# Six stacked layers on one core: keys ahead of the norm spreads, the hidden products a slot later, GELU behind both squares

## The reference, cut to what matters

```python
def attn_layer(x, Wqkv, qs, ksc, Wo):          # 16 heads of 64, windows of 32 keys
    q, k, v = split(x @ Wqkv)
    q = l2norm(q) * qs; k = l2norm(k) * ksc
    q, k = rotary(q), rotary(k)                 # k with the inverse scale
    sim = q @ k.T * 8, this window and the one before, masked
    return softmax(sim) @ v @ Wo
def ffn_layer(x, g, bln, W1, b1, W2, b2):
    xn = (x - mean) / sqrt(var + 1e-5) * g + bln
    a, gate = split(xn @ W1 + b1)               # 341 columns each, padded to 3 x 128
    return a * gelu(gate) @ W2 + b2
x = attn_layer(shift_tokens(x)) + x
x = ffn_layer(shift_tokens(x)) + x
```

## Time and profile before

| | |
|---|---|
| median of 3 runs | 4278.9 us (4273.93 to 4289.5) |
| profiled execution, own time | 4266.5 us |
| its span | 4264.8 us, mean granted TensorE clock 0.96 |
| TensorE matmul busy | 3939.0 us (92%) |
| VectorE busy | 3159.2 us (74%) |
| ScalarE busy | 3038.3 us (71%) |
| GpSimd busy | 1809.0 us (42%) |

### The profile page before, as it was taken

The page is one execution under the profiler, slowest core; times in us unless marked ns, Lnnn a source line. Parts: engine busy times, 40 slices in busy tenths (PEclk is TensorE's granted clock), DMA queues, the critical chain, the costliest instruction groups (busy, mean ns, idle before and its releaser), DMA issues. The chain is left out here.

```text
span 4264.8 us, 112685 instructions
## 1 busy us (share of the span) xinstructions
PE 3939.0 (92%) x43857; PEld 2386.4 (56%) x43857; DVE 3159.2 (74%) x4169; ACT 3038.3 (71%) x7076; POOL 1809.0 (42%) x1071
## 2 busy tenths in 40 slices
PE   7997999999999999999967589999999999999997
PEld 3443666656555655556536446565566565665664
DVE  5774878878877877778735478778778787887785
ACT  3555777777778777777762267787777777777876
POOL 3112444444444444444404534444444444444442
PEclk8998999999999999999986699999999999999999
DMA  2212444444444444444300044444444444444442
GB/s 44 32 22 74 104 112 104 109 106 99 110 104 95 113 103 103 108 103 103 75 11 3 3 122 108 111 96 114 104 95 111 100 109 98 107 107 103 96 103 50
DMA packets 232525, 380.84 MB, mean 89 GB/s; under 512 B 59364, under 2 KB 122336, under 8 KB 231688
## 3 DMA queue, kind: packets, MB, share of 16 engines
q1 hardware_dynamic: 231560, 372.20, 37.5%
q10 hardware_dynamic: 384, 0.79, 0.1%
HBM read 39.22 MB, written 1.05 MB: 9 GB/s over the span
## 5 line engine op out<-in xcount | busy, mean ns | idle before, releaser
L839 POOL TENSOR_TENSOR b_roll<-b_roll,b_sws 128x1024 f32<-128x1024 f32 x384 | 910.1, 2370 | 1741.0 <-DMA b_sws<-b_roll 1741.0
L1205 DVE SCALAR_TENSOR_TENSOR b_roll<-ps,b_qks,b_rot 128x1024 f32<-128x1024 f32 x768 | 956.3, 1278 | 109.5 <-ACT b_sq L1135 72.3
L1120 ACT ACTIVATE b_prob<-ps,b_nmx 128x96 f32<-128x96 f32 x3072 | 756.0, 374 | 0.7 <-DVE b_nmx L1226 0.2
L1253 DVE TENSOR_TENSOR b_roll<-b_roll,ps 128x512 f32<-128x512 f32 x384 | 264.1, 688 | 503.1 <-PE ps L942 498.0
L844 POOL TENSOR_TENSOR b_prob<-b_prob,b_rinv 128x768 f32<-128x768 f32 x384 | 566.1, 1474 | 119.7 <-DVE b_rinv L1267 118.6
L881 PEld LDWEIGHTS ps<-ident,b_prob 128*128 128x128 f32 x3072 | 381.4, 142 | 309.6 <-issue 254.2
L881 PE MATMUL ps<-ident,b_prob 128*128 128x128 f32 x3072 | 468.3, 275 | 49.9 <-issue 28.4
L1072 ACT ACTIVATE b_pT<-ps 128x512 f32<-128x512 f32 x768 | 488.5, 636 | 29.1 <-PE ps L881 28.5
L1012 PE MATMUL ps<-b_wqkv,b_xs 128*128 128x256 f32 x1536 | 408.3, 388 | 35.0 <-DVE b_roll L1205 34.9
L934 PE MATMUL ps<-b_oT,b_wo 128*128 128x512 f32 x768 | 405.7, 610 | 14.7 <-ACT b_oT L1087 12.0
L903 PEld LDWEIGHTS ps<-b_pT,b_vs 128*64 128x64 f32 x6144 | 310.1, 137 | 184.2 <-issue 159.9
(11 more groups left out here) (290 smaller groups left out, 6956.9 us busy)
## 6 DMA issues: line engine op xcount, KB each, us to landing
b_sws<-b_roll SPq DMA_DIRECT2D x1536, 128.0 KB, 2.3
b_vs<-b_va SPq DMA_DIRECT2D x384, 256.0 KB, 3.8
b_wqkv<-in_L_ffn_Wqkv SPq DMA_DIRECT2D x96, 192.0 KB, 3.6
b_xs<-y SPq DMA_DIRECT2D x126, 128.0 KB, 2.3
b_wo<-in_L_ffn_Wo SPq DMA_DIRECT2D x96, 64.0 KB, 3.2
b_xs<-y SPq DMA_DIRECT2D x42, 127.8 KB, 2.4
b_rot<-in_rot SPq DMA_DIRECT2D x2, 2048.0 KB, 8.0
b_w<-in_L_ffn_W SPq DMA_DIRECT2D x24, 170.5 KB
```

The costliest lines, as they stand in the source:

```text
L839: pool.tensor_tensor(prc[:, r, :, :], prc[:, r, :, :], sws[:, r % 2, :, :], ALU.add)\
L1120: g = act.activation(prob[:, kc, i, P - KEYS:P], wide[0][:, h * CH + m * KEYS:h * CH + (m + 1) * KEYS], ACT.Exp, bias=nmx[:, kc % 2, i:i + 1])
L1205: dve.scalar_tensor_tensor(out=two_runs((2 * r + i) * CH, (8 + 2 * (r % 2) + i) * CH), in0=both, scalar=scale, in1=rot[:, 2 * i:2 * i + 2, ...
```

## The change

It moves work between places in the order of each engine; no operation is added or taken away, and every shape stays.

- TensorE: the keys of a come right after Wo, ahead of the two spreads, and the queries after the spreads. The spread for q goes to bank 2 and that for k to bank 7, where before they went to banks 1 and 2. The strips go to bank 2 instead of bank 6. The hidden products a (L965) run in steps 3 to 5 instead of 2 to 4; the products g stay in 2 to 4.
- ScalarE: the square of the keys comes before that of the queries, both behind the exponentials and ahead of the second transposes and of the GELU. The square for the variance, the second half of the LayerNorm's inverse root, and the bias of the normalised input move behind the exponentials.
- VectorE: the sum of the probabilities and its reciprocal move from the end of a slot to the start of the next; the hidden bias add goes between them and the rotary products; the sum into y moves ahead of the normalised q; the normalised input of the feed-forward comes last.

```diff
@@ TensorE @@
-                    if step in (2, 3, 4):
-                        pe.wait_ge(S["f_acp"], ONE + FT * C + step - 1)
+                    if step in (3, 4, 5):
+                        pe.wait_ge(S["f_acp"], ONE + FT * C + step - 2)
...
-                def strips(U, d, pe=pe):
+                def strips(U, b, pe=pe):
                     pe.wait_ge(S["sqk_done"], ONE + U + 1)
-                    if d:
-                        pe.wait_ge(S["pt_cp"], ONE + 2 * um(d)[0] + 2)
+                    pe.wait_ge(S["sqq_done"], ONE + U + 1)
+                    if b:
+                        pe.wait_ge(S["qn_done"], ONE + um(b)[0] + 1)
                     for s in range(4):
-                        m = pe.matmul(bank[6][32 * s:32 * s + 32, :], head_of[:, :], sq[:, s, :],
+                        m = pe.matmul(bank[2][32 * s:32 * s + 32, :], head_of[:, :], sq[:, s, :],
...
+                        if p:
+                            pe.wait_ge(S["pk_done"], ONE + um(p)[0] + 1)
+                        pe.matmul(bank[1][:, :], W[:, 1, :], X, start=True, stop=True).then_inc(S["k_mm"], 1)
+                    if b:
+                        UB, kb = um(b)
+                        pe.wait_ge(S["split_done"], ONE + twos(b) + 1)
+                        key_bank_free(f0)
+                        if j % 2 == 0 and p:
+                            pe.wait_ge(S["ln_done"], ONE + twos(p) + 1)
+                        pe.matmul(bank[2][:, :], take[:, 2 * (kb % 2), :], rsp[:, :], start=True, stop=True)
+                        if e:
+                            pe.wait_ge(S["y_add"], ONE + UE + 1)
+                        pe.matmul(bank[7], take[:, 2 * (kb % 2) + 1, :], rsp[:, :], start=True, stop=True)\
+                            .then_inc(S["nb_mm"], 1)
+                    if a:
                         pe.wait_ge(S["va_cp"], ONE + U)
                         pe.matmul(bank[0][:, :], W[:, 0, :], X, start=True, stop=True).then_inc(S["q_mm"], 1)
...
                     if d:
+                        if b:
+                            pe.wait_ge(S["kn_done"], ONE + UB + 1)
                         values(d, 0)
                         values(d, 1)
-                    if step in (0, 1, 2, 3, 4) and b:
-                        pe.wait_ge(S["kn_done"], ONE + UB + 1)
+                    if step in (0, 1, 2, 3, 4):
+                        if b:
+                            pe.wait_ge(S["qn_done"], ONE + UB + 1)
+                        if a and j % 2:
+                            pe.wait_ge(S["ln_done"], ONE + twos(a) + 1)
@@ ScalarE, order of a slot after the change @@
 o_cp; Ln of the variance or copy of g; values; turned(0); table; 8 exponentials;
 Exp of the inverse root; square of the variance; square of k; square of q; bias of the input;
 turned(1); table and GELU; inverse norms (odd slots)
@@ VectorE, order of a slot after the change @@
 sum and reciprocal of d; hidden add (before in 3, 4, 5); rotary q, rotary k; maximum of c_;
 output add; centring; split (even); y_add; qn from bank 2; kn from bank 7; norm (step 2)
```

More of the change, by code:

```diff
@@ L970, in slot @@
                         m.then_inc(S["f_out"], 1)
[L971 to L974, removed]
-                            pe.wait_ge(S["pk_done"], ONE + um(p)[0] + 1)
-                        pe.matmul(bank[1][:, :], W[:, 1, :], X, start=True, stop=True).then_inc(S["k_mm"], 1)
                     if b:
@@ L1212, in slot @@
                     ok, OC = ffn_out(f0)
+                    if d:
+                        UD, kd = um(d)
+                        dve.wait_ge(S["exp_done"], ONE + UD + 1)
+                        dve.tensor_reduce(ssm[:, kd % 2, :], prob[:, kd, :, P - KEYS:P], AX.X, ALU.add)\
+                            .then_inc(S["ssum_done"], 1)
+                        dve.wait_ge(S["ssum_done"], ONE + UD + 1)
+                        dve.reciprocal(rinv[:, kd % 2, :], ssm[:, kd % 2, :]).then_inc(S["rinv_done"], 1)
+                    if before in (3, 4, 5):
+                        i = before - 3
+                        dve.wait_ge(S["f_a"], ONE + FT * C0 + i + 1)
+                        dve.tensor_scalar(hid[:, i, :], bank[3][:, :], b1[:, 0, i:i + 1], None, ALU.add).then_inc(S["f_acp"], 1)
                     if p:
@@ L1226, in slot @@
                         dve.tensor_reduce(nmx[:, kc % 2, :], sc, AX.X, ALU.max, negate=True).then_inc(S["smax_done"], 1)
+                    if ok is not None:
+                        dve.wait_ge(S["f_out"], ONE + OC + 1)
+                        dve.scalar_tensor_tensor(out=y[:, cs(ok)], in0=bank[3][:, :], scalar=b2[:, 0:1], in1=y[:, cs(ok)],
+                                                 op0=ALU.add, op1=ALU.add).then_inc(S["y_done"], 1)
+                    if before == 0:
+                        dve.wait_ge(S["f_mean"], ONE + C0 + 1)
+                        dve.tensor_tensor(fin, xs[:, cs(fk0)], bank[2][:, :], ALU.subtract).then_inc(S["f_cen"], 1)
+                    if b and j % 2 == 0:
+                        n = twos(b)
+                        dve.wait_ge(S["rn_done"], ONE + n + 1)
+                        dve.scalar_tensor_tensor(out=rsp[:, :], in0=rhi[:, :].bitcast(F32), scalar=minus_hi[:, 0:1], in1=rn[:, :],
+                                                 op0=ALU.mult, op1=ALU.add).then_inc(S["split_done"], 1)
+                    if e:
+                        UE, ke = um(e)
+                        ys = y[:, cs(chunk(e))]
+                        dve.wait_ge(S["wo_mm"], ONE + UE + 1)
+                        dve.tensor_tensor(ys, bank[7], ys, ALU.add).then_inc(S["y_add"], 1)
+                    if b:
+                        UB, kb = um(b)
+                        dve.wait_ge(S["add_done"], ONE + UB + 1)
+                        dve.wait_ge(S["nb_mm"], ONE + UB + 1)
+                        dve.tensor_tensor(prc[:, kb, 0, :], prc[:, kb, 0, :], bank[2][:, :], ALU.mult).then_inc(S["qn_done"], 1)
+                    if b:
+                        at = PAD + (kb % 2) * CH
+                        dve.tensor_tensor(kr[:, at:at + CH], prc[:, kb, 1, :], bank[7], ALU.mult).then_inc(S["kn_done"], 1)
                     if step == 2:
```

89 lines of the change are left out of this document (22 added, 67 removed).

## The result

The changed kernel takes 4338.66 us in the median of 4 runs (4334.44 to 4344.65). The kernel before, with one more run of its own, takes 4280.96 us (4273.93 to 4289.5). The ratio is 1.0139 (95%: 1.0116 to 1.0161), so the change costs 58 us. The profiled execution took 4335.23 us, with a span of 4333.5 us against 4264.8. The direction was forecast, the size was not: 4302 us, with 4332 as the upper end.

A forecast was written before the change was run, and what follows sets the result against it. TensorE was taken as full except where it waits for other engines. +1.25 us a layer gave 15 us, first layers +6, unloaded weights +2: +23, 4290, scaled to a 4302 us median; range 4262 to 4332.

The forecast's parts named there:

- -0.60: Slots 5, 11, 21, 27: lose 0.86 us of hidden product, gain the uncovered 0.26; -2.40 us a layer.
- Part 2: Hidden product a slot later: -0.60 in four slots, +0.53 in four GELU slots; worth about nothing.
- Parts at nothing: Probabilities' sum, ScalarE's feed-forward pieces, satisfied waits and bank 2's strips (Ln cover 0.2 us) were to cost nothing.
- The rest of the sum: All forecast terms together: +23 us on the profiled execution's 4266.5 us.
- 1.25: Net forecast slowdown per layer, in us; 15 us in 12 layers.
- 6 for the first layers: Each stack's first layer lacks feed-forward work in slots 3 to 15: 3.4 us instead of 0.4, +6 for two stacks.
- Keys ahead, +0.26: Keys before the spreads delay the normalised k and the mask: 0.26 us in each uncovered slot, +0.14 left in 10 and 26.
- y earlier: Sum into y starts 1.13 us sooner, removing transfer waits: -0.30 in slot 19, -0.39 in slot 22.
- GELU's slots: Slots 8, 14, 24, 30 take the 0.86 us hidden product; +0.53 each, +2.12 for four.
- Shared banks: Rival: k spread waits for the sum into y in bank 7; 0.2 us late gives 4340 us; chance 0.13.
- The reverse: Rival: normalised k's lateness not exposed, mask at W+3.58 instead of 3.84, some 4245 us; chance 0.12.

The follow-up runs named there:

- e1: Changed kernel, with GpSimd's add of the rotated half waiting for VectorE's feed-forward norm in step 2; 4289.7 us, ratio 1.0025 to the kernel before.
- e3: Changed kernel, with the norm's second factor read from the keys' bank in PSUM instead of the inverse root in SBUF; 4288.56 us, ratio 1.0022.
- e9: Changed kernel, with the norm back ahead of the sum into y and the inverse root's second half back behind its Ln; 4296.06 us, ratio 1.0025.
- e5: Kernel before, with only VectorE's sum into y moved ahead of the normalised q; 4250.19 us, ratio 0.9934.
- e12: Changed kernel with e1's wait, but TensorE's order, banks, ScalarE's squares and the probabilities' sum as in the kernel before; 4237.27 us, ratio 0.9884.
- e11: Kernel before, with y's sum ahead of the normalised q, hidden products a slot later, ScalarE's bias behind the keys' square; 4234.63 us, ratio 0.9885.
- e7: Kernel before, with only the hidden products and their bias add a slot later; 4279.39 us, ratio 1.0013.
- e2: Changed kernel, with ScalarE's bias of the normalised input behind the second transposed copy instead of ahead of it; 4332.45 us, ratio 1.0122.

## Why the prediction was too low

**The step that failed** is the -0.60 for slots 5, 11, 21 and 27 in Part 2, which measured +0.86, +0.71 and +0.79 in three of the four, and behind it "Parts at nothing". That part costs VectorE's reorder by the sum of the probabilities alone and never prices the norm's move behind kn, although the change lists it. The move takes the norm from a place where it never met GpSimd's add (44 of 44 at a mean of 0.752 us in the kernel before) to one where, in 36 of 44, it is caught by the add. e1, e3 and e9 each remove the overlap, or its condition, in a different way, and all give back 37 to 50 us of span. By the slots: slots 5 and 11 have the norm in 10 layers, 27 in 12, and slot 21 is caught in 4 of 12 (10.61 to 10.82 us, against 9.13). That makes 10 x (1.46+1.31) + 12 x 1.39 + 4 x 1.59 = 51 us, and e1's span is 48.7 under that of the change. With the term in it the sum would have been 23+51 = +74 us, where the span grew by 68.7.

**The rest of the sum** came out at +20.0 us in e1's span where +23 was forecast, but this agreement is partly luck. I took ten whole layers, from the first normalised q of a layer to that of the next, leaving out the last layer of each stack and the passages:

| | ten layers, us | to before |
|---|---|---|
| before | 2883.4 | |
| after | 2922.5 | +39.1 |
| e1 (add waits for the norm) | 2890.3 | +6.9 |
| e5 (sum into y alone) | 2865.7 | -17.7 |
| e12 (e1 without the keys' move) | 2851.0 | -32.4 |
| e11 | 2848.2 | -35.2 |

The forecast for these ten is 10 x 1.25 + 6 for the first layers + 0.8 for the weights not loaded in them = +19.3, and e1 has +6.9. Of this the two first layers have +10.3, about the 9.3 of the sum, and the eight inner ones -3.5 instead of +10. The rest of e1's +20 lies in the passages and the last layers, to which the sum gave almost nothing. How much of that belongs to the change is open: the stack's first normalised q stands anywhere from 402.64 to 418.88 us in the profiled executions of all kernels, behind a stage that none of the kernels changes. Point by point:

- *Keys ahead, +0.26.* Seven of the eight slots named with +0.26 have +0.23 to +0.26; slot 2 has +0.56, and slots 10 and 26, forecast at +0.14, have +0.22 and +0.21. Its reason was half right. kn does hold the mask after the change. Of the order before, it said that the chain has no slack; e12 shows that with y out of the chain kn has 0.63 us to spare and TensorE alone keeps the mask at 3.57. The 0.26 at the mask is real all the same (3.84 against 3.57 with y first in both). But in even slots the keys' move also takes away what y first would give: slot 16 is 8.16 us in e1 and 7.49 in e12.
- *y earlier.* Forecast -0.30 and -0.39, measured -0.42 and -0.52. The forecast read one layer, while these two slots differ by layer in the kernel before: 8.94 to 10.21 us for 19 and 8.80 to 9.63 for 22 in the inner layers. By e5 the move alone gives 0.7% in the kernel before; no case of the forecast had it by itself. The -0.43 to -0.46 of slots 9, 15 and 25 isn't of this move, which alone makes them 0.41 longer: it comes with the later hidden product (e7 alone has slot 9 at 11.51).
- *GELU's slots.* Forecast +0.53, measured +0.82, although the next W came where forecast (8.20 against 8.30). The slot was 7.30 from values product to values product, and I had worked from 7.77, Wo to Wo. The wait at its end that the 7.77 held belongs in this measure to the next slot, and there its going shows as part of the -0.46. From Wo to Wo slot 8 went from 7.77 to 8.20, +0.43.
- *Shared banks.* They did not bind: the k spread stood at W+1.95 or 1.96 in most slots and at 2.06 in slots 16 and 18, and TensorE's own wait for y there stands in the profile 4 times, 2.2 us in all. That this rival's 4340 us lies beside the measured 4339 is chance. Its price was also too high by the forecast's own count: it takes 192 slots, where the sum and the next rival have about 150, which gives 4332. What bank 2 costs appeared only in e2, 0.86 us behind a late bias.
- *The reverse* is excluded by the mask at 3.84. e12 is 1.2% faster, but it isn't this rival: it does not move the keys, and its mask at 3.57 is only where it was before. It gains in the even slots, as e5, and in slots 5, 11, 21 and 27, at 9.14 instead of 9.72.

Slot 21 shows how thin the margin is. There the add waits for its transfer 5.49 to 6.06 us in the 8 layers where the norm wins, and 5.22 to 5.43 us in the 4 where it loses. What makes the transfer later in the 8 I did not try to find out.

## What to carry to other kernels

When an instruction changes its place, look at what the other engines do at the new place, by their rows of the same slot, even if its own duration and its cover are known. Here a VectorE instruction with both tensors in SBUF that began while GpSimd ran a long one lost 1.7 to 2.2 us each time, and a wait that made GpSimd start second left slots 5, 11 and 27 at 9.13 to 9.16 us, as forecast. Look in the profile before at the least, median and most of each line: one line with two durations, whose ends keep a fixed distance to another engine's, is held by that engine, although no wait shows it. A product taken out of a slot gives back only what the other engines' lateness in that slot leaves of it, so measure each part of a reorder alone. The best parts here were small moves (the sum into y, and the bias that makes the later hidden products pay), and the largest one (the keys) used up what they gave.

## What the runs showed of the hardware

- A 128x512 f32 scalar_tensor_tensor on VectorE with both tensors in SBUF takes 0.745 us alone. When GpSimd's 128x1024 f32 tensor_tensor (2.37 us) has already begun, it ends 0.55 us after that one ends, whatever was left of it (2.46 to 2.94 us in 34 of 34, and in two that began 0.01 and 0.03 us ahead). GpSimd's own time does not change then (2.36 to 2.38 us).
- The same instruction with one tensor in PSUM takes 0.748 us in the middle of the same add.
- Who begins first decides, and then the other one pays. Where the norm began 0.09 to 0.13 us ahead, it took 0.75 us and the add 2.86 to 2.90 instead of 2.37; where it began 0.5 us ahead or more, the add took 2.39 to 2.50. Being first by 0.01 and by 0.03 us was not enough (norm 2.92 and 2.94); in e2 0.07 us was (norm 0.745, add 2.91). The pair from a slot 21 of the changed kernel:

```profile
1156.77 0.75 DVE L1272 SCALAR_TENSOR_TENSOR cen<-cen,b_lng,sqr 128x512 f32<-128x512 f32 x1
1156.86 2.90 POOL L839 TENSOR_TENSOR b_roll<-b_roll,b_sws 128x1024 f32<-128x1024 f32 x1 [5.50 <-DMA b_sws<-b_roll]
```

- VectorE's split of the inverse norm has two tensors in SBUF too. It is 0.750 us in the median and up to 1.231 us in the changed kernel. There 16 of 192 overlap GpSimd's scaling of the probabilities, and the 9 that take over 0.76 us all end 0.55 us after it; in the kernel before it was 13 of 13, behind the scaling (128x768) or the add.
